# Side probabilities turned by TensorE in wrapped 64-column blocks, up to slot 35 of a fused attention and recurrent FFN kernel

## The reference

```python
# layer 1: attention with 16 heads of 32, window of 64 keys on both sides
scores = einsum('bhqd,bhkd->bhqk', qh, kh) / sqrt(32)      # q = layernorm(x), k = v = ctx_1024
scores = where(abs(i - j) > 64, -inf, scores)
x = x + softmax(scores) @ vh @ W_proj.T + b_proj
# layer 2: a gated recurrence over the batches, state of 512 x 512
for b in range(8):
    f, i = sigmoid(xt @ wf.T + c @ uf.T + bf), sigmoid(xt @ wi.T + c @ ui.T + bi)
    c = f * c + i * tanh(xt @ wc.T + c @ uc.T + bc)
x = x + tanh(einsum('tbi,oi->tbo', x2, wo) + c @ uo.T + bo)  # x2 = layernorm(x)
```

## Time and profile before

| | |
|---|---|
| median of three runs | 943.76 us (943.57 to 945.68) |
| profiled execution, first to last instruction (the time shown for it) | 941.8 us |
| median less that span | 1.96 us |
| PE busy | 918.6 us (98%) |
| DVE busy | 676.1 us (72%) |
| ACT busy | 476.5 us (51%) |
| POOL busy | 204.8 us (22%) |

### The profile page before, as it was taken

How to read it: one execution, slowest core, us unless ns; L and a number is a source line. 1 busy time by engine, 2 the same in 40 slices (tenths; PEclk the granted TensorE clock), 3 DMA queues, 4 the chain that set the end, 5 groups by cost and what they waited for, 6 DMA issues and landing times.

```text
span 941.8 us, 21981 instructions
## 1 busy us (share of the span) xinstructions
PE 918.6 (98%) x7842; PEld 715.5 (76%) x7842; DVE 676.1 (72%) x2281; ACT 476.5 (51%) x1430; POOL 204.8 (22%) x228
## 2 busy tenths in 40 slices
PE   7999999899999999999999999999999999999998
PEld 5555567678877788887887888788877888878887
DVE  6888898788779977998799878987798531143222
ACT  6888666655455544645565555555655321131222
POOL 5475322211101111111111111111101100003444
PEclk9999999999999999999999999999999999999999
DMA  9464232234444453544443444433333150059862
GB/s 305 161 192 150 88 96 69 87 89 126 135 111 134 119 143 96 135 110 124 130 141 112 121 114 122 115 107 110 97 98 91 50 163 0 1 179 382 307 237 101
DMA packets 139348, 123.58 MB, mean 131 GB/s; under 512 B 46824, under 2 KB 104168, under 8 KB 137704
## 3 DMA queue, kind: packets, MB, share of 16 engines
q1 hardware_dynamic: 138520, 121.91, 42.6%
q10 hardware_dynamic: 720, 0.27, 0.2%
HBM read 87.70 MB, written 34.46 MB: 130 GB/s over the span
## 4 chain that ended last, share of the span: by engine, by line
PE 85%; DVE 6%; issue 3%; ACT 2%; DMA 2%; POOL 1%; SPq 0%; DVEq 0%; ACTq 0%; POOLq 0%
PE ps_g L684 18%; PE ps_g L686 17%; PE ps_g L685 17%; PE ps_a L731 5%; PE ps_a L753 4%; PE ps_m L684 3%; PE ps_v L774 3%; PE ps_m L686 3%; PE ps_m L685 3%; PE ps_m L806 2%; PE ps_a L684 2%; PE ps_v L779 2%; DVE probs L1013 2%; PE ps_a L686 2%; PE ps_a L685 2%
## 5 line engine op out<-in xcount | busy, mean ns | idle before, releaser
L901 ACT ACTIVATE probs<-probs,rowmin 128x192 f32<-128x192 f32 (+1 forms) x512 | 239.4, 470 | 114.3 <-DVE rowmin L1013 114.3
L1013 DVE CUSTOM_DVE_ANT_0 probs<-ps_a,mask 128x192 f32<-128x192 f32 (+1 forms) x512 | 166.1, 386 | 31.7 <-PE ps_a L731 30.6
L684 PE MATMUL ps_g<-state_hi,gate_w 128*128 128x512 f32 x336 | 133.6, 398 | 0.0
L686 PE MATMUL ps_g<-state_hi,gate_w 128*128 128x512 f32 x336 | 131.1, 390 | 0.0
L685 PE MATMUL ps_g<-state_lo,gate_w 128*128 128x512 f32 x336 | 130.9, 389 | 0.0
L1048 DVE STREAM_TRANSPOSE keys<-probs 32x128 f32<-32x128 f32 x420 | 125.6, 299 | 5.2
L948 ACT ACTIVATE gate<-ps_g,bias 128x512 f32<-128x512 f32 x84 | 57.6, 686 | 105.7 <-PE ps_g L686 105.2
L901 ACT ACTIVATION_READ_ACCUMULATOR probs<-probs,rowmin 128x1 f32 x512 | 96.3, 188 | 0.0
L663 POOL TENSOR_TENSOR attn_lo<-recip,attn_hi 128x512 fp32r<-128x512 f32 x23 | 29.8, 1294 | 276.8 <-ACT attn_hi L914 276.8
L906 ACT ACTIVATE probs_t<-ps_a 128x512 f32<-128x512 f32 x108 | 59.3, 595 | 52.3 <-PE ps_a L753 52.3
L684 PE MATMUL ps_g<-x2t_even,gate_w 128*128 128x512 f32 x192 | 80.0, 417 | 0.0
(11 more groups left out here) (211 smaller groups left out, 1722.4 us busy)
## 6 DMA issues: line engine op xcount, KB each, us to landing
values<-ctx_rows SPq DMA_DIRECT2D x34, 256.0 KB, 4.3
xr<-x SPq DMA_DIRECT2D x32, 256.0 KB, 3.8
keys<-ctx_t SPq DMA_DIRECT2D x16, 512.0 KB, 4.2
x_dram<-xr SPq DMA_DIRECT2D x32, 256.0 KB, 2.6
gate_w<-x2t_dram SPq DMA_DIRECT2D x8, 1024.0 KB, 9.8
keys<-ctx_t SPq DMA_DIRECT2D x16, 384.0 KB, 3.4
x2t_dram<-x2t_even SPq DMA_DIRECT2D x12, 512.0 KB, 4.1
x2t_dram<-x2t_odd SPq DMA_DIRECT2D x12, 512.0 KB, 4.4
```

The source lines that it names most:

```text
L684: pe.matmul(ps, lhs[0], rhs[0], start=start, stop=False)
L686: return pe.matmul(ps, lhs[1], rhs[0], start=False, stop=stop)
L901: act.activation(row, row, ACT.Exp, bias=rowmin[:, i % 2, h:h + 1], scale=-1.0, accum_out=rowsum[:, i // G % 2, i % G, h:h + 1]).then_inc( ...
L1013: dve.tensor_tensor_reduce(probs[:, i % 2, h, 0:SEEN[t]], ps_a[h][:, score_at[i]:score_at[i] + SEEN[t]], mask[:, MASK0[t]:MASK0[t] + SEEN[ ...
```

## The change

Up to slot 35 there is one scheme. PE turns the own keys as before in four transposes, and right after them, in the same `turn` step, the side keys:

- Inner tiles up to tile 6 (1, 2, 5 and 6: 16 slots, `wrapped`). A query sees only one side: the first 64 queries the left one, the last 64 the right one. So 64 columns hold the sides of all 128 queries. Even heads keep them behind the own keys, odd heads ahead, so that the side blocks of two heads lie next to each other and one 128x128 transpose turns both: two transposes to a slot. Rows of `probs` are 192 columns for DVE's mask and ACT's exponential, where they were 256. The scores of a slot take twelve matmuls (four of 192, four of 128, four of 64 columns) where they took eight of 192. The mask is a new tile, made by POOL with a memset and four `affine_select` in a new step behind `recip` of slot 0. The values of the two sides are each loaded twice, into both halves of the partitions, the right ones into a tile of their own.
- Edge tiles (0, 3, 4, 7 and 8: 20 slots). Four transposes of 64x64.

DVE copies 256 columns of PSUM instead of 512 (up to slot 19) or of its own block transposes (slots 20 to 35). The bank of the turned sides is `ps_g[1]` up to slot 19 and `ps_a[1]` after. In `value` the sides take matmuls of 64 columns over 64 partitions, four for an edge and eight for an inner tile; before it was four of 128 columns (up to slot 19, and inner tiles after) or of 64 columns over 128 partitions (edge tiles from slot 20). `score` of slot i now also waits for the copy of the sides of slot i-2, and `turn` for the masks of two heads of the next slot instead of one.

```diff
+    def wrapped(i):
+        return i < SENT and len(SIDE_HALVES[i % TT]) == 2
+    def row_cols(n, h):
+        if wrapped(n // G):
+            return slice(WINDOW, KEYS) if h % 2 == 0 else slice(0, ROW)
+        return slice(0, SEEN[n // G % TT])
...
-            if n + 1 >= OWN_BANKS:
+            if n + 1 >= FIRST_TWO:
                 steps.append(("sides", n + 1))
...
+                        for a in SIDE_HALVES[t]:
+                            first = KEY0[t] + SIDE_COL[t][a]
+                            rows = ctx_rows[b, first:first + WINDOW, :]
+                            if wrapped(i):
+                                sp.dma_start(side_values(i, a), rows.unsqueeze(0).to_broadcast([PAIR, WINDOW, D]))\
+                                  .then_inc(v_in[i % 2], DMA)
...
+            def turn_sides(i):
+                t = i // G % TT
+                if wrapped(i // G):
+                    for h in range(0, HPG, PAIR):
+                        at = KEYS * h + ROW
+                        mm = pe.transpose(ps_sides[i][:, WINDOW * h:WINDOW * h + P], prob_rows[i % 2][:, at:at + P], ident[:, :])
+                else:
+                    a = SIDE_HALVES[t][0]
+                    q, k = slice(WINDOW * a, WINDOW * (a + 1)), slice(SIDE_COL[t][a], SIDE_COL[t][a] + WINDOW)
+                    for h in range(HPG):
+                        mm = pe.transpose(ps_sides[i][0:WINDOW, WINDOW * h:WINDOW * (h + 1)], probs[q, i % 2, h, k], ident[q, q])
+                mm.then_inc(turned_2, 1)
+            def score_wrapped(i):
+                tile, g = i // G, i % G
+                for a in range(2):
+                    q = slice(WINDOW * a, WINDOW * (a + 1))
+                    for part in range(2):
+                        for h in range(HPG):
+                            rows = slice(HEAD * h, HEAD * (h + 1))
+                            whole = h % 2 != a
...
+                            mm = pe.matmul(ps_a[h][q, to], queries[rows, g, q], keys[rows, key_home[tile], g, k],
+                                           start=True, stop=True)
+                mm.then_inc(scored, 1)
...
                         if i - 2 >= OWN_BANKS:
                             pe.wait_ge(turned_a, i - 1)
+                            pe.wait_ge(turned_b, i - 1)
...
-                        for c in range(2):
-                            some = min(SEEN[i // G % TT] - c * P, P)
-                            for h in range(HPG):
-                                pe.wait_ge(expd, HPG * i + h + 1)
-                                mm = pe.transpose(ps_g[c][0:some, h * P:(h + 1) * P],
-                                                  probs[:, i % 2, h, c * P:c * P + some], ident[:, :])
-                            mm.then_inc((turned, turned_2)[c], 1)
-                        continue
-                    if i >= FIRST_TWO:
+                    elif i >= FIRST_TWO:
                         pe.wait_ge(masked, HPG * (i - i % 2 + 2))
                     else:
-                        pe.wait_ge(masked, HPG * (i + 1) + 1)
+                        pe.wait_ge(masked, HPG * (i + 1) + 2)
...
                     mm.then_inc(turned, 1)
+                    if i < FIRST_TWO:
+                        turn_sides(i)
...
+                    if i < FIRST_TWO:
+                        for a in SIDE_HALVES[tile % TT]:
+                            q = slice(g * P + WINDOW * a, g * P + WINDOW * (a + 1))
+                            for h in range(HPG):
+                                d = slice(g * P + HEAD * h, g * P + HEAD * (h + 1))
+                                rows, cols = side_of(i, h, a)
+                                mm = pe.matmul(ps_v[HEAD * h:HEAD * (h + 1), q], side_values(tile, a)[rows, d],
+                                               turned_sides[rows, cols], start=False, stop=(a == SIDE_HALVES[tile % TT][-1]))
+                        mm.then_inc(valued, 1)
+                        continue
...
-                if kind == "turn" and i < OWN_BANKS:
-                    some = min(SEEN[i // G % TT] - P, P)
+                if kind == "turn" and i < FIRST_TWO:
+                    rows = slice(0, P) if wrapped(i // G) else slice(0, WINDOW)
                     dve.wait_ge(turned_2, i + 1)
                     need(dve, valued, i)
-                    dve.tensor_copy(probs_t[0:some, HPG:2 * HPG, :],
-                                    ps_g[1][0:some, :].rearrange("p (a q) -> p a q", a=HPG)).then_inc(turned_b, 1)
+                    dve.tensor_copy(turned_sides[rows, 0:HPG * WINDOW], ps_sides[i][rows, 0:HPG * WINDOW]).then_inc(turned_b, 1)
```

More of the change, by code:

```diff
@@ L154, in bass_xattn_ffn @@
     steps += [("ln1", 0), ("ln1b", 0), ("bias", 0), ("query", 0), ("query_out", 0)]
-    steps += [("score", 0), ("ln1", 1), ("score", 1), ("exp", 0), ("recip", 0)]
+    steps += [("score", 0), ("ln1", 1), ("score", 1), ("exp", 0), ("recip", 0), ("wrap_mask", 0)]
     SPLIT_AT = {1: [0], 2: [1], G: [2, 3], 2 * G: [4, 5, 6], 3 * G: [7, 8, 9], 4 * G: [10, 11]}
@@ L476, in bass_xattn_ffn, with side_values, side_of @@
         x2t_home[0] = x2t_home[B - 2]
+        ps_sides = [ps_g[1] if n < OWN_BANKS else ps_a[1] for n in range(FIRST_TWO)]
+        turned_sides = probs_t[:, HPG:2 * HPG, :].rearrange("p a q -> p (a q)")
+        prob_rows = [probs[:, r].rearrange("p h k -> p (h k)") for r in range(2)]
+        def side_values(i, a):
+            return right_v[i % 2] if wrapped(i) and a == 1 else values[:, i % 2, 1]
+        def side_of(i, h, a):
+            if wrapped(i // G):
+                rows = slice(WINDOW * (h % PAIR), WINDOW * (h % PAIR + 1))
+                at = P * (h // PAIR) + WINDOW * a
+            else:
+                rows, at = slice(0, WINDOW), WINDOW * h
+            return rows, slice(at, at + WINDOW)
         ps_turn = [ps_g[0] if n < OWN_BANKS else ps_a[n % 2 if n >= FIRST_TWO else 0] for n in range(SLOTS)]
@@ L722, in _ @@
                             pe.wait_ge(turned_a, i - 1)
+                            pe.wait_ge(turned_b, i - 1)
+                    if wrapped(tile):
+                        score_wrapped(i)
+                        continue
                     if i == 0:
@@ L761, in _ @@
                         need(pe, attn_t, tile)
[L762 to L771, removed]
                     for h in range(HPG):
@@ L1011, in _ @@
                         dve.wait_ge(turned_b, i - 1)
+                    if wrapped(i // G):
+                        dve.wait_ge(wrap_consts, 5)
                     for h in range(HPG):
-                        dve.tensor_tensor_reduce(probs[:, i % 2, h, 0:SEEN[t]],
-                                                 ps_a[h][:, score_at[i]:score_at[i] + SEEN[t]],
-                                                 mask[:, MASK0[t]:MASK0[t] + SEEN[t]], -SCALE, -NEG, ALU.add, ALU.min,
+                        if wrapped(i // G):
+                            seen, masks = ROW, wrap_mask[:, row_cols(i, h)]
+                        else:
+                            seen, masks = SEEN[t], mask[:, MASK0[t]:MASK0[t] + SEEN[t]]
+                        dve.tensor_tensor_reduce(probs[:, i % 2, h, row_cols(i, h)],
+                                                 ps_a[h][:, score_at[i]:score_at[i] + seen],
+                                                 masks, -SCALE, -NEG, ALU.add, ALU.min,
                                                  rowmin[:, i % 2, h:h + 1]).then_inc(masked, 1)
```

60 lines of the change are left out of this document (44 added, 16 removed).

## The result

The changed kernel takes 961.78 us (median of four runs, 958.79 to 962.15); the kernel before took 943.66 us beside it (942.75 to 945.68). The ratio is 1.0187, with a 95% interval of 1.0175 to 1.0200: slower by 18 us. The forecast was 942.7 us with a range of 937 to 949, so the forecast and the range both missed. The profiled execution spans 956.9 us.

A forecast was written before the change was run, and what follows sets the result against it. PE was taken to bound the kernel, with DVE and ACT nearly full up to slot 19. The terms 10.6 - 8.2 - 0.5 - 3.0 = -1.1 us took 943.8 to 942.7 us, range 937 to 949.

The forecast's parts named there:

- What waits newly: Scores waiting for DVE's side copy just fit, nothing charged, at worst 4 x 0.4 us; added side loads under 1 us.
- DVE's relief: Smaller copies and dropped block transposes, slots 0 to 35: DVE loses some 26 us, 16 to 18 in slots 20 to 35.
- Turning: PE's transposes from slot 20: inner +0.24 us per slot; edge 0.36 plus two height changes of 0.13.
- Value steps: One more change of tile height on PE: +0.13 us per inner slot and per edge slot from slot 20.
- Wrapped scores: Inner slots' score matmuls on PE: +0.2 us each, floor +0, ceiling +0.5, as the second half of queries queues.
- Sum on PE, slots 20 to 35: Added PE work: inner 0.57 x 8 = 4.6, edge 0.75 x 8 = 6.0, together +10.6 us (floor 3.9, ceiling 16).
- What comes back there: Slots 20 to 35: 2.5 us of PE's waits vanish and 5.7 us are filled by new work, 8.2 us in all.
- The wait of 96.68: PE waits 1.45 us for `mult`, behind DVE's memset and six block transposes; all 1.45 us goes.
- Slots 0 to 19: PE's work changes by -0.5 us and 3.0 us (1 to 5) of its waits come back.
- nothing of the new work fills a wait: Slower rival, slots from 20 on: exponential waits stay as long, +5.7 us, 948.4 us; chance 0.20.
- the relief is not on the path: Slower rival: PE's waits are all ACT's, POOL's and the DMA's, so only filling counts, 948.2 us; chance 0.06.
- Near their floor: Faster rival: PE's additions near minimum, 3.9 us in slots 20 to 35; 933.4 us, 938 taken as its time; chance 0.38.

The follow-up runs named there:

- The runs with 2, 4, 8 and 16: Kernel before plus two unused 256 KB broadcast loads ahead of the weights, leading dimension 2, 4, 8 or 16: 952.44, 950.94, 947.06, 943.38 us.
- the pair without a stride of zero: Kernel before plus two unused 256 KB loads with a leading dimension of 2 whose halves are different rows: 952.56 us, ratio 1.0103.
- the changed kernel with plain loads: Changed kernel, each side block of values of an inner tile loaded by two DMAs of 64 rows instead of one broadcast DMA: 943.05 us, ratio 1.0000.
- the two other traces of the old scheme: Kernel before plus two unused 256 KB loads, sent as four plain DMAs of 64 rows (943.02 us) or as broadcasts of sixteen (943.38 us).
- the three versions with plain loads in all tiles: Changed kernel with plain side loads throughout (943.05 us), and the same with the new scheme only up to slot 27 (940.61 us) or 19 (941.47 us).
- the version up to slot 27: Changed kernel with plain side loads, edge tiles of slots 28 to 35 as in the kernel before: 940.61 us, ratio 0.9974.

## Why the prediction was wrong

**The step that failed** is the last of "What waits newly": "SyncE issues one more load for tiles 1 and 2, and 256 KB more ahead of the weights at the start: under 1 us at some 300 GB/s, before weights for which ACT isn't seen waiting." The load was priced by its bytes. The bytes are indeed free (943.02 against 942.96 us); the price is set by the form, a destination and a source whose leading dimension is 2. It is 13.2 to 13.4 us until a pair has landed, a delay of the weights queued behind (`u_c` landed 18.5 us after its issue, 9.2 in the kernel before), and a fall of the clock on top: some 18 us in all where under 1 was charged. The remark that ACT isn't seen waiting was true and gave no margin: in the kernel before, ACT began with these weights at 17.2 us, in the changed one they landed at 26.2. No rival had this mechanism, and the slower rivals near 948 were right in sign for wrong reasons.

The Trainium skill has the rule (page DMA: Bandwidth & Descriptors, section Why a DMA increments its semaphore by 16 and not by 1, and again in Rules for kernel authors): the number of DMA engines that share a transfer is the largest up to 16 that divides the leading dimension of both sides, so a leading broadcast of c copies is confined to c engines at most. The runs with 2, 4, 8 and 16 (ACT's wait 8.5, 5.0, 2.3 and none) agree with it, and so does the pair without a stride of zero. The share of 0.13 in the changed kernel's windows, two engines' worth of 16, is what the rule gives for a leading dimension of 2. For 4 and 8 no window has such a load by itself. The rule stood against the change and was not weighed.

**The rest of the sum** can be held against the changed kernel with plain loads, 943.05 us; the forecast of 942.7 is what that kernel takes, within its interval. That is partly luck: in the stretches below the work of PE was charged 2.4 us too high, and what comes back was put 1.2 us too high in slots 20 to 35 and the gain up to slot 19 1.1 too high, so the errors cancel. Part by part:

- *DVE's relief*: right. The copies of 256 columns take 0.38 to 0.43 us (0.41 forecast), and DVE lost 19.0 us in the second stage (16 to 18).
- *Turning*: right. Inner +0.22 (0.24 forecast). Edge +0.54 (0.36 + 0.13 + 0.13 = 0.62), so the 64x64 transposes and the two changes of height are a little cheaper together. The four transposes stand as x4 in the trace and take 0.34 us with a change of height, so no further passes show.
- *Value steps*: right. +0.14 for an inner slot (0.13). The change of height of 0.13 us was real.
- *Wrapped scores*: wrong in size. +0.20 was charged, 0.05 at most measured (0.53 against 0.48 for the shortest ones before): twelve small matmuls, x24 in the trace, take about as long as eight, x16. The floor held nearly. The premise that the second half of the queries waits behind two others in a tile didn't show.
- *Sum on PE, slots 20 to 35*: 8 x 0.36 + 8 x 0.67 = 8.2 us (8.6 with 0.05 for the scores), 10.6 forecast.
- *What comes back there*: the stretch is 1.2 us longer, so 7.0 us came back, 8.2 forecast (against the two other traces of the old scheme it is 1.9 and 2.1 us longer, and 6.1 to 6.3 came back). It is unevenly spread, which the forecast didn't say: inner slots were given 2.9 us of work and got 1.5 us shorter, edge slots 5.4 us and got 2.7 to 3.6 longer. The wait of 96.68 is gone, as said. The premise was too large: the prediction put PE's idle time in this stage at 11.5 us, but in the earlier trace rows it is 95.00 less 87.65, 7.35 us, less than the 8.2 that were to come back. In slots 20 to 35 it fell from 6.5 to 0.4 us; nothing was left to fill.
- *Slots 0 to 19*: -2.1 to -2.4 us in the traces of the three versions with plain loads in all tiles, -3.5 forecast. The list of waits has POOL's `recip` at 56 us still (1.40 us with plain loads, 1.16 in the earlier trace rows); the relief of DVE runs into it.
- *New waits*: rightly charged nothing. With plain loads PE's list of waits from 92 to 190 us has no copy of sides in it.
- *Rivals*: "nothing of the new work fills a wait" and "the relief is not on the path", both at 948, are out by the same kernel. "Near their floor", 938, is right on the scores alone; the changes of height stayed, and so did the time. The effect that it promised came only when the edge slots from 28 on were left out, 940.6.

The prediction also said that time gained before slot 36 reaches the end one for one. Of the 3.8 us that the version up to slot 27 was ahead there, 1.9 did in the profiled execution and 2.4 in the median.

What stays open: what a late weight costs without the fall of the clock; no run kept the one without the other. The late weights further on (`w_i` landed 10.55 us after its issue) show as no added idle time of PE in the changed kernel's slots 0 to 19: outside of the wait of 9.48 it idled 6.8 us, with plain loads 7.4 outside of the 0.64. Nor was a version tried with the broadcast loads moved behind the weights.

## What to carry to other kernels

Read the shape of every added DMA, not only its bytes: here a pair of transfers whose outermost dimension is two took three times as long as plain ones and delayed what was queued behind it, and two plain transfers in place of each, or a broadcast of sixteen, cost nothing that could be measured. When all engines of a stretch are less busy and the clock has fallen, look for one late transfer before looking for too much work. And price a scheme for each kind of slot by itself: here it paid up to slot 27 and cost on the edge tiles behind it, and the mixture showed as no change.

## What the runs showed of the hardware

- The second of two DMAs of 256 KB with a leading dimension of 2 landed 13.2 to 13.4 us after its issue, where plain ones of this size have a median of 4.4. While the pair was in flight the DMA share was 0.13 at 51 GB/s. Sixteen copies as leading dimension cost nothing that can be measured (ratio 1.0003).
- A slow transfer holds up the engine that issues: single issues by SyncE took 4.07 us (`x_dram`) and 5.33 us (`w_c`) behind it, where the same issues took 0.43 and 1.93 us in the kernel before.
- After PE had stood for 5.6 and 9.0 to 9.5 us the granted clock was 0.50. It stayed there for 10 us of renewed full work after the 5.6, for 4 after the 9.0 and for some 12 after the 9.5 (the changed kernel), so the length of the stop doesn't order them. After the wait of 2.9 us with eight copies it was 0.90 and 0.67 in the two windows that follow.
- Score steps with x24 small matmuls in tiles of 32x64 took 0.53 us from start to start, those with x16 and the same columns in sum 0.48 at the least.
